# Two accumulators from tile 59 on and three from tile 48; two loaded and added while tiles run; rows without a token left out of the scatters

## The reference, cut to what matters

```python
logits = jnp.einsum('th,eh->te', x.astype(jnp.float32), gate_w.astype(jnp.float32))
scores = jax.nn.softmax(logits, axis=-1)
topk_w, topk_ids = jax.lax.top_k(scores, TOP_K)           # TOP_K = 6, 64 experts
topk_w = topk_w / (jnp.sum(topk_w, axis=-1, keepdims=True) + EPS)
comb = comb.at[jnp.arange(T)[:, None], topk_ids].add(topk_w.astype(x.dtype))
gu = jnp.einsum('th,efh->tef', x, w_gate_up)
g, u = (gu[..., :FFN], gu[..., FFN:])                     # FFN = 176
act = jax.nn.silu(g) * u
act = act * comb[:, :, None]
routed = jnp.einsum('tef,ehf->th', act, w_down)           # [1024, 256]
return routed + shared                                    # then x = x + this
```

## Time and profile before

| | before |
|---|---|
| median of 3 runs | 294.2 us (292.29 to 294.91) |
| profiled execution: its own time | 293.05 us |
| its span, first to last instruction | 291.2 us |
| mean granted TensorE clock | 0.973 |
| PE busy | 258.4 us (89%) |
| POOL busy | 178.2 us (61%) |
| DVE busy | 150.3 us (52%) |
| ACT busy | 126.2 us (43%) |
| scatters to accumulators | 70, 1.55 us of POOL each |
| weight loads | 71 of 496 KB and 71 of 48 KB |

### The profile page before, as it was taken

The page is one execution under the profiler, slowest core; times in us unless marked ns, Lnnn a source line. Parts: engine busy times, 40 slices in busy tenths (PEclk is TensorE's granted clock), DMA queues, the critical chain, the costliest instruction groups (busy, mean ns, idle before and its releaser), DMA issues.

```text
span 291.2 us, 6600 instructions
## 1 busy us (share of the span) xinstructions
PE 258.4 (89%) x1674; PEld 225.5 (77%) x1674; DVE 150.3 (52%) x696; ACT 126.2 (43%) x374; POOL 178.2 (61%) x155
## 2 busy tenths in 40 slices
PE   6998758888889879999999999999999999999810
PEld 4695436666656669999999999999999999999700
DVE  3834897799996744544433333333333333334355
ACT  2524433332322544555555555555555555555300
POOL 9301257767776734677877667776766665577600
PEclk9999997799999999999999999999999999999995
DMA  6999999999943638999999999999999999988597
GB/s 162 393 429 430 417 361 377 390 399 387 382 173 134 202 85 198 334 327 352 351 353 333 332 321 325 330 325 321 327 323 329 332 332 334 335 184 161 77 322 260
DMA packets 50632, 89.08 MB, mean 306 GB/s; under 512 B 6578, under 2 KB 37379, under 8 KB 49571
## 3 DMA queue, kind: packets, MB, share of 16 engines
q1 hardware_dynamic: 29714, 63.75, 60.9%
q0 software_dynamic: 12816, 17.12, 27.6%
q10 hardware_dynamic: 8064, 7.80, 7.9%
HBM read 58.11 MB, written 30.54 MB: 304 GB/s over the span
## 4 chain that ended last, share of the span: by engine, by line
PE 66%; DVE 17%; DMA 7%; issue 4%; POOL 3%; ACT 2%; SPq 0%; POOLq 0%; DVEq 0%; ACTq 0%
PE PS L1188 29%; PE PS L1200 10%; PE PS L1201 10%; PE PS L1057 5%; PE PS L1140 3%; DVE M L888 2%; DMA VXG<-x_slots 2%; DMA XN<-acc 2%; DVE X L979 2%; POOL x_slots L449 2%; PE PS L1020 2%; DMA acc<-PT,IDR 2%; PE PS L1014 1%; PE PS L1027 1%; PE PS L1035 1%
## 5 line engine op out<-in xcount | busy, mean ns | idle before, releaser
L1188 PEld LDWEIGHTS PS<-XT,WA 128*128 128x128 f32 (+1 forms) x852 | 105.5, 187 | 5.0 <-ACT XNT L556 0.8
L1188 PE MATMUL PS<-XT,WA 128*128 128x128 f32 (+1 forms) x852 | 106.0, 274 | 1.0 <-ACT XNT L556 0.6
L492 POOL DMA_INDIRECT acc<-PT,IDR x52 | 81.0, 1558 | 37.5 <-ACT PT L660 17.3
L934 DVE TENSOR_TENSOR AC<-SG,PS 128x128 f32<-128x128 f32 x71 | 20.4, 288 | 95.6 <-ACT SG L628 95.2
L660 ACT ACTIVATE PT<-PS,WT 128x256 f32<-128x256 f32 x70 | 33.1, 473 | 34.4 <-PE PS L1201 33.7
L446 POOL DMA_INDIRECT x_slots<-HX,SLOT x36 | 35.1, 976 | 16.0 <-issue 9.6
L1200 PE MATMUL PS<-WA,AC 128*128 128x256 f32 x140 | 41.8, 381 | 0.0
L1201 PE MATMUL PS<-WB,AC 128*128 128x256 f32 x140 | 41.7, 379 | 0.0
L492 POOL DMA_INDIRECT out_rows<-PT,IDR x18 | 28.1, 1561 | 14.9 <-ACT PT L660 6.9
L549 ACT COPY XT<-PS 128x256 f32<-128x256 f32 x73 | 27.1, 372 | 19.8 <-PE PS L1057 17.4
L627 ACT ACTIVATE SG<-PS 128x128 f32<-128x128 f32 x71 | 19.7, 277 | 27.8 <-PE PS L1188 27.8
(11 more groups left out here) (154 smaller groups left out, 310.1 us busy)
## 6 DMA issues: line engine op xcount, KB each, us to landing
WA<-in_wa SPq DMA_DIRECT2D x71, 496.0 KB, 13.7
x_slots<-WA SPq DMA_DIRECT2D x1, 8704.0 KB, 28.7
VXG<-x_slots ACTq DMA_DIRECT2D x56, 136.0 KB, 6.6
WB<-in_wb SPq DMA_DIRECT2D x71, 48.0 KB, 16.4
acc<-ZERO SPq DMA_DIRECT2D x2, 1152.0 KB, 18.9
VXG<-x_slots SPq DMA_DIRECT2D x8, 136.0 KB, 2.2
CT<-in_ctxT SPq DMA_DIRECT2D x2, 512.0 KB, 6.1
X<-in_x SPq DMA_DIRECT2D x2, 512.0 KB, 6.2
```

The lines of the kernel that those rows point to most:

```text
L492: pool.indirect_dma_start(acc[j], bass.IndirectOffsetOnAxis(ap=IDR[:, u:u + 1], axis=0), YS[:, u % YR, :], None, compute_op=ALU.add).then_ ...
L934: v.tensor_tensor(AC[:, w % 2, 0, :], SG[:, w % 2, 0, :], PS[:, 4 + w % 2, 0:128], ALU.mult)
L1188: last = mm(PS[0:n, (4 if c == 2 else 2) + w % 2, c % 2 * 128:(c % 2 + 1) * 128], WA[:, base:base + n], XT[:, w % 2, k, :], start=(k == 0) ...
```

## The change

A table `STAGES` takes the place of the two constants. Tiles 0 to 47 use accumulators 0 to 3 in turn as before; tiles 48 to 58 use 1, 2, 0; tiles 59 and up use 0, 1. The last tile on acc 3 is therefore 47, on acc 2 it is 58, on acc 1 it is 68 and on acc 0 it is 69. SP loads them in the order 3, 2, 1, 0, and holds at most two pieces of 3 and 2 in flight. VectorE adds 3 into 2, the late product into 2, 2 into 1, 1 into 0. The scatters get a bound on the row number, 1023, above which a row is left out without an error.

```diff
--- before.py
+++ after.py
@@ -50,8 +50,7 @@
 SEED = float(0x5f3759df - 2 ** 31)
 ZROWS = 8
 STEPS = B + 5
-RETIRE = 60
-LATE_ACC = (1, 2, 0)
+STAGES = ((0, (0, 1, 2, 3)), (48, (1, 2, 0)), (59, (0, 1)))
 KEPT = B - 2
 
 P_BANK, V_BANK, SCORE = (2, 3, 6, 7), (4, 5, 0, 2), (3, 6)
@@ -233,11 +232,12 @@
 
         def home(t):
 
-            return t % NACC if t < RETIRE else LATE_ACC[(t - RETIRE) % len(LATE_ACC)]
+            first, ring = max(stage for stage in STAGES if stage[0] <= t)
+            return ring[(t - first) % len(ring)]
 
         def on_home(t):
 
-            return t // NACC if t < RETIRE else RETIRE // NACC + (t - RETIRE) // len(LATE_ACC)
+            return sum(home(w) == home(t) for w in range(t))
 
         def tile_landed(eng, i, n):
 
@@ -248,11 +248,13 @@
 
         def scattered(eng, K, j):
 
-            if j in LATE_ACC:
-                late = (K + (E - RETIRE + len(LATE_ACC) - 1 - LATE_ACC.index(j))) * 43 // 128
-                eng.wait_ge(s_acc[j], late * 16 + 16 * (RETIRE // NACC))
+            first, ring = STAGES[-1]
+            early = 16 * sum(home(w) == j for w in range(first))
+            if j in ring:
+                late = (K + (E - first + len(ring) - 1 - ring.index(j))) // len(ring)
+                eng.wait_ge(s_acc[j], late * 16 + early)
             else:
-                eng.wait_ge(s_acc[j], 16 * (RETIRE // NACC))
+                eng.wait_ge(s_acc[j], early)
 
         def sum_in(eng, j, c, landed):
             here, rows = piece_rows(j, c)
@@ -378,7 +380,11 @@
                 if c >= 2:
                     sp.wait_ge(s_sum3[c - 2], 16)
                 sum_in(sp, 3, c, s_sum3)
-            for j, landed in ((2, s_sum2), (0, s_sum0), (1, s_sum1)):
+            scattered(sp, K, 2)
+            for c in range(MC):
+                sp.wait_ge((s_sum3 + s_sum2)[c + 2], 16)
+                sum_in(sp, 2, c, s_sum2)
+            for j, landed in ((1, s_sum1), (0, s_sum0)):
                 scattered(sp, K, j)
                 for c in range(MC):
                     sum_in(sp, j, c, landed)
@@ -491,7 +497,8 @@
                 pool.sem_inc(s_turn)
                 pool.indirect_dma_start(acc[j],
                                         bass.IndirectOffsetOnAxis(ap=IDR[:, u:u + 1], axis=0),
-                                        YS[:, u % YR, :], None, compute_op=ALU.add).then_inc(s_acc[j], 16)
+                                        YS[:, u % YR, :], None, compute_op=ALU.add,
+                                        bounds_check=N - 1, oob_is_err=False).then_inc(s_acc[j], 16)
 
             for u in range(U):
                 step(0, u)
@@ -986,11 +993,11 @@
             dve.wait_ge(s_tail, B - KEPT)
             need(tick(v.tensor_tensor(piece(2, MC - 1), piece(2, MC - 1), PS[:, 0, 0:MW], ALU.add)))
             for c in range(MC):
-                dve.wait_ge(s_sum0[c], 16)
-                n = tick(total(0, 2, c))
+                dve.wait_ge(s_sum1[c], 16)
+                n = tick(total(1, 2, c))
             need(n)
             for c in range(MC):
-                dve.wait_ge(s_sum1[c], 16)
+                dve.wait_ge(s_sum0[c], 16)
                 total(0, 1, c).then_inc(s_sum, 1)
```

## The result

| | before | changed |
|---|---|---|
| median | 294.56 us (292.29 to 296.05, 4 runs) | 298.02 us (295.82 to 299.05, 4 runs) |
| profiled execution | 293.05 us | 299.05 us |
| its span | 291.2 us | 297.2 us |
| tile 47's scatter starts | 221.81 | 222.78 |
| tile 58's scatter starts | 248.34 | 254.74 |

The changed kernel is slower by 1.4%: its time is 1.014 times that of before, with a 95% interval of 1.0086 to 1.0194. The forecast was 291.1 us; the second rival's time was 297.9.

The account below looks back on a forecast made before the run. TensorE was taken to bound the loop at 2.41 us a tile, a 3 MB transfer the end. Span 291.2 - 3.1 gain + 0 cost = 288.1 us, profiled 289.95, median forecast 291.1 us; range 288.8 to 296.5.

Parts of the forecast that it names:

- What bounds the kernel: Tile loop: TensorE never stops, 2.41 us a tile; what ends last is the 3 MB load transfer beginning at 274.53.
- The gain: End of the kernel: two accumulators' loads leave it, so the last piece is taken up 3.1 us earlier.
- The forecast's fast bound: In the gain at the end: 2.0 us for tile 68's landing gives 283.0 and a gain of 4.5 us.
- The cost of three accumulators: Scatters of tiles 48 to 58: fewer rows bring the distance to about 7.0 us, so no growing delay.
- The unhelped figure: Tiles 48 to 58 without help from left-out rows: scatters 5.7 us late at tile 58.
- The cost of two accumulators: From tile 59: up to 2 us delay in tiles 59 to 63, 3 us won back in 64 to 69.
- The quiet distance: Start-to-start distance on one accumulator from tile 59: 4.39 us landing plus about 0.7 until POOL starts, 5.1 us.
- Rival 1: Scatters: part of the delay stays, tile 69 starts 1 to 4 us late, end at 292 to 295; 28%.
- Rival 2: Scatters: left-out rows aren't those that end the scatter; 8.46 us stays, delay 6.8 us, time 297.9 us; 13%.
- The rule weighed there: Skill's descriptor swizzle, for direct transfers: DMA engines 0 to 7 serve partitions 0 to 63, eight each.
- Rival 3: Scatters: skipped rows are still sent somewhere, 7.2 us late, time 298.3 us; 4%.
- Rival 4: POOL: the check makes it slow; at 3.1 us an instruction 70 us more, 361 us; 5%.

Follow-up runs that it names:

- the two patterns above: Changed kernel with rows of partitions 64 to 127 counted empty: 296.69 us, 1.012 of before; with 32 to 63 and 96 to 127 empty instead: 290.87 us, 0.9889.

## Why the prediction was wrong, point by point

**What bounds the kernel** was right: TensorE's 2.41 us a tile did not change, and the end is scatter, load, sum, store.

**The gain** had the right mechanism and came out a fifth smaller. Tile 68's landing was taken at 3.4 us and took 3.1 (280.66 to 283.78); tile 69's at 4.1 and took 4.3 (283.39 to 287.68). From acc 0's issue to its last piece's sum it was taken as 5.4 and took 6.1 (287.68 to 293.77, the second of the two in the row at 293.10). The gain was 2.5 us instead of 3.1. The sums of 3 and 2 are hidden, as said. It is limited by the last load's own way: from its issue to the end the span takes 9.5 us, and took 10.3 before (280.86 to 291.2). The loads that were removed had been running mostly beside tile 69's scatter, not behind it: acc 2's were issued from 274.53 on, and that scatter landed at 280.86. The variant without a delay, with the rows of partitions 0 to 31 and 64 to 95, gained 2.6 us, which agrees. The forecast's fast bound was no bound: with tile 68 landed in 2.0 us, acc 0's own 284.35 still stood, and 283.0 needed a faster tile 69 too.

**The cost of three accumulators: the step that failed.** "With 30% fewer rows: 8.46 - 0.30 x 6.2 = 6.6, or 8.46 - 0.30 x 3.4 = 7.4", then "I take about 7.0: no growing delay". Measured: 8.7 to 9.0 us. Both bounds rested on one assumption, that the landing shrinks with the number of rows. It goes by the last of the 16 increments, 7.7 us after the start on average over tiles 48 to 56 against 7.8 before. Leaving out 30% of the rows did not move it, because the rows left out are those in the high partitions; of the rows in 0 to 63, which by the two patterns above set the landing, all are there in a tile of 64 tokens or more. The unhelped figure stood beside it and was right: 5.7 us late at tile 58, measured 5.4.

**The cost of two accumulators** was mis-sized in its recovery. The quiet distance was taken as 5.1 and is 5.0 to 5.7 in tiles 59 to 63 of this trace and up to 6.5 in the later one of the same kernel. "3 us in all" were to be won back from tile 64 on; nothing was: 7.2 us at tile 64, 7.6 at tile 69. Scatters of 5 to 49 rows still land 3.1 to 4.3 us after their start, which with 0.8 to 0.9 us until POOL starts is 4 to 5 us for two tiles' 4.82, and the gather of 1.0 us stands in between. POOL's pace of 1.85 us was the limit only twice.

**The rivals.** Rival 1, given 28%, fell short: it had tile 69 1 to 4 us late. Rival 2, given 13%, is what happened: its sign, a distance of 7.6 us or more, came at 8.7 to 9.0. That its time, 297.9, is so near to 298.02 is luck: in the traces the delay was 7.6 us instead of 6.8 and the gain 2.5 instead of 3.1, a loss of 5.1 us and not 3.7, while the medians are 3.5 apart. The rule weighed there spoke against the change and was set aside because "the other engines are relieved". The semaphore records agree that part of the scatter is done sooner (the first increment after 3.9 us instead of 6.8), and it does not help. Rival 3 (the rows are still sent) holds in a weak form: the packets remain, but are small. Rival 4 is out: POOL's instruction is 1.57 us on average, and 1.56 before. The wait for tile 72's gather occurred as described, 2.4 us, off the path, since tile 69's scatter waits for tile 67's.

## What to carry to other kernels

A scatter landed here with the last of its 16 increments; leaving out rows helped only where the partitions that set it lost some, so ask which partitions the useful rows lie in before pricing it by their number. A ring of accumulators has a distance (here landing plus 0.8 to 0.9 us), and dividing it by the tile's time gives the number that is needed: 3.6 under weight traffic and 2.1 to 2.4 in the quiet end here. Before paying with a shorter ring for transfers moved off the end, ask how much of them already ran beside the last thing that is waited for.

## What the runs showed of the hardware that was not expected

A row left out by the bound of an indirect scatter is not removed from the transfer: the number of packets is the same, and it counts among those under 512 B (2,816 of them, to the row). POOL's time for the instruction does not change with it (1.55 us with 128 rows or with 5). A scatter of 5 or 8 rows in the quiet end still needs 3.1 us to land, against 3.7 to 4.4 for 128 rows (tiles 65 to 68 before). With the same limit of 64 rows, two patterns of partitions differ by 2.0 us in landing (7.8 and 5.8 us on average over tiles 48 to 56) and by 5.8 us in the kernel's time.
